# Counting the ranks of a router on VectorE instead of TensorE, in a one-core transformer block

## The chip, the cores and the metric

The kernel runs on one core of a Trainium2 chip. The metric is the device time of one execution in microseconds (us), lower is better. Five engines work side by side, each with its own in-order queue: TensorE (PE in the rows; PEld is its weight load), VectorE (DVE), ScalarE (ACT), GpSimd (POOL) and SyncE (SP, which here only starts transfers). They wait for one another through semaphores.

## What is computed

A transformer block on 8 batches of 512 tokens with 256 features: an adaptive layernorm, an attention block, a second layernorm, and a feed-forward part that ends in five steps of a spiking neuron. The attention has a light branch (windows of 64 tokens, all tokens) and a heavy branch (256 routed query tokens against 256 routed key tokens). What matters for the change is the routing: each token gets a score, and the 256 tokens with the largest scores are picked, in the order of their scores.

```
def route(rt, num):
    scores = jnp.einsum('bnd,d->bn', x, rt)
    idx = jnp.argsort(scores, axis=-1)
    ...
    sel_s, sel_i = (cs[:, -num:], idx[:, -num:])
    sel_s = sel_s + jax.lax.stop_gradient(1.0 - sel_s)
    return (sel_s, sel_i)
sq, iq = route(rt_q, NQ)
skv, ikv = route(rt_kv, NKV)
rq = jnp.take_along_axis(x, iq[:, :, None], 1)
rkv = jnp.take_along_axis(x, ikv[:, :, None], 1)
```

There are two routings for each batch (queries, r = 0, and keys, r = 1), 16 in all. The selected scores come out as 1, so only the token numbers count.

## The kernel before

The program is software-pipelined by hand. Its main part is a row of iterations, one for each batch: a "first" one, six equal ones ("loop", batches 1 to 6) and a "last" one, then a tail. An iteration has 24 slots, one for each pair of heads and block of queries (slots 0 to 15 light, 16 to 23 heavy; the last iteration has another order). In every slot each engine does its part of the attention, and then what tables put into that slot for other work:

- TensorE: the score products two slots ahead (`scores`), the units of the slot, the transposes of the probabilities (`turn`, L1243), and the products with the values of the slot before (`attend`).
- VectorE: `invert` (L1509), `minimum` (L1499 to L1503), `copy_out` (L1516), its share of the units, and then the row stages of the slot.
- ScalarE: a copy of the transposed probabilities, the exponentials, its share of the units, and the normalisation.
- GpSimd: gathers and scatters of rows by token number, reciprocal roots, and a few elementwise parts, at slots named in `POOL_SLOTS`.

`turn` of slot s waits for `copy_out` in slot s of VectorE, so the two engines can't drift apart by more than about a slot. A slot's end on TensorE comes either when its own products are through or when `copy_out` is.

The tables `FIRST_UNITS`, `SLOT_UNITS` and `LAST_UNITS` name the units of each slot. K, Q, V and NK, NQ, NV are projections of the light branch (6 products, L1059), HQ, HK, HV those of the heavy branch, FC and YA the two halves of the feed-forward part (L1059, L1190; FD is VectorE's part of it), LO and HO output projections (L1113, L1118), HT, ZT and Z3 transposes (L1091, L1123, L1128; Z3 turns the normalised rows of the feed-forward part), WF and WP preparations of weights. Units other than FD and YA share two PSUM banks, which alternate in the order of the table; a unit that is next for a bank waits until its last user is drained. `FIRST_ROWS`, `ROW_STAGES` and `LAST_ROWS` name VectorE's row stages: `stats1`, `center`, `modulate`, `add`, `stats3`, `norm3` and so on.

The routing for the next batch goes through these steps, each in a slot given by the tables: `router` (VectorE, four reductions to scores), SR (TensorE spreads the scores over all partitions, ScalarE copies them to `score_row`), `compare` (VectorE: for each of the four token tiles one row block of 0 and 1 of greater or equal, and a small one for ties, 11 instructions in two stages a and b), RK (TensorE sums these blocks over the partitions by 20 products with a column of ones, so the ranks land in PSUM), VectorE's part of RK (ranks to SBUF, then four instructions that mark, for each place of 256, which token holds it: `spots`), IX (TensorE: 16 products of `spots` with the token numbers, split in a low and a high part so that they are exact), VectorE's copy to `picks`, and then GpSimd's `pick`, which gathers the rows. The gathered rows are needed by HT at the start of the next iteration.

## Time and profile before

| | |
|---|---|
| median of 3 runs | 890.96 us (890.9 to 891.18) |
| the profiled execution: its own time | 887.45 us |
| the profiled execution: span from first to last instruction | 885.4 us |
| mean granted TensorE clock in it | 0.984 of full speed |

The profiled execution ran 3.5 us below the median of the timed runs, and its span is 2.05 us shorter than its own time; what lies outside the span belongs to the start and the end of the execution.

### The profile page before, as it was taken

Reading aid. Unit: us, or ns where it says so; the run is one execution under the profiler, and the core shown is the slowest. Engines: PE = TensorE matmul, PEld = TensorE weight load, DVE = VectorE, ACT = ScalarE, POOL = GpSimd, SP = SyncE. Lnnn points to the kernel's source line nnn. Section 1 sums busy time; section 2 is a strip of 40 time slices with the busy share of each in tenths; the row PEclk is TensorE's granted clock in tenths of the full one; section 3 lists DMA queues with packets and bytes.
Section 4 is the critical chain, followed back from the end, with each engine's and each line's share of the span. In section 5 each row is a group of like instructions: output and inputs, shape, how many; then the busy total and the mean of one; then the engine's idle time right before and its main releaser. Section 6 shows DMA issues by size and latency. Waiting matters only on the chain.

```text
span 885.4 us, 23955 instructions
## 1 busy us (share of the span) xinstructions
PE 820.1 (93%) x9170; PEld 622.8 (70%) x9170; DVE 586.1 (66%) x1740; ACT 612.7 (69%) x1738; POOL 206.5 (23%) x267
## 2 busy tenths in 40 slices
PE   4786889999999999999999999999999999999976
PEld 1464667678776777778776777677776777767766
DVE  6586763786568756786567756786567766453565
ACT  2355676788667886788667876787767886688633
POOL 3103021220241224120331224120222223200343
PEclk9798999999999999999999999999999999999998
DMA  9400030200022001310022000320022000210110
GB/s 317 148 31 26 4 100 13 91 26 2 26 75 82 25 14 39 102 54 2 26 67 91 25 14 25 97 67 8 21 71 91 25 14 25 61 49 1 37 31 24
DMA packets 32847, 45.35 MB, mean 51 GB/s; under 512 B 3304, under 2 KB 28144, under 8 KB 32512
## 3 DMA queue, kind: packets, MB, share of 16 engines
q1 hardware_dynamic: 29616, 37.53, 12.9%
q0 software_dynamic: 2304, 6.29, 2.3%
q8 instruction: 74, 1.21, 0.6%
q14 instruction: 37, 0.30, 0.1%
q10 hardware_dynamic: 816, 0.00, 0.0%
HBM read 32.52 MB, written 14.97 MB: 54 GB/s over the span
## 4 chain that ended last, share of the span: by engine, by line
PE 76%; DVE 6%; ACT 3%; issue 2%; POOL 1%; DVEq 0%; POOLq 0%; ACTq 0%
PE ps_unit L1059 30%; PE ps_y L1190 10%; PE ps_turned L1243 7%; PE ps_unit L1113 5%; PE ps_scores L1217 4%; PE ps_turned L1265 4%; PE ps_turned L1280 4%; PE ps_unit L1118 3%; PE ps_scores L1226 3%; DVE hn L1474 1%; PE ps_turned L1270 1%; DVE spikes L1491 1%; PE ps_unit L1123 1%; PE ps_unit L1152 1%; DVE loT L1516 1%
## 5 line engine op out<-in xcount | busy, mean ns | idle before, releaser
L990 ACT ACTIVATE probs<-ps_scores,row_min 128x192 f32<-128x192 f32 (+2 forms) x384 | 161.1, 425 | 101.5 <-DVE row_min L1499 54.0
L1000 ACT ACTIVATE probs<-probs,row_inv 128x192 f32<-128x192 f32 (+2 forms) x384 | 155.6, 456 | 0.4 <-DVE row_inv L1509 0.4
L1059 PE MATMUL ps_unit<-xT,wqkv 128*128 128x512 f32 x384 | 109.3, 422 | 2.7 <-POOL xT L798 1.7
L1499 DVE TENSOR_REDUCE row_min<-ps_scores 128x2 f32<-128x512 f32 (+1 forms) x128 | 78.6, 614 | 49.9 <-PE ps_scores L1226 24.3
L1243 PEld LDWEIGHTS ps_turned<-ident,probs 64*128 64x128 f32 x1280 | 56.0, 139 | 75.2 <-issue 65.6
L1190 PE MATMUL ps_y<-wprojT,hid_parts 128*128 128x256 f32 x768 | 104.2, 284 | 1.4 <-POOL hid_parts L563 0.9
L1190 PEld LDWEIGHTS ps_y<-wprojT,hid_parts 128*128 128x128 f32 x768 | 96.5, 188 | 10.0 <-issue 5.8
L1243 PE MATMUL ps_turned<-ident,probs 64*128 64x64 f32 x1280 | 81.5, 238 | 21.5 <-DVE loT L1516 19.1
L1059 PEld LDWEIGHTS ps_unit<-xT,wqkv 128*128 128x128 f32 x384 | 70.8, 194 | 29.5 <-issue 15.5
L1059 PE MATMUL ps_unit<-h_parts,wfcT 128*128 128x512 f32 x336 | 90.1, 403 | 0.1
L1008 ACT ACTIVATE probsT<-ps_turned 128x384 f32<-128x384 f32 x128 | 61.9, 484 | 21.9 <-PE ps_turned L1270 21.9
L990 ACT ACTIVATION_READ_ACCUMULATOR probs<-ps_scores,row_min 128x1 f32 x384 | 75.5, 197 | 0.0
L1217 PE MATMUL ps_scores<-kT,qT 64*64 64x192 f32 (+1 forms) x1024 | 71.3, 320 | 4.0 <-ACT probs L990 3.2
L1516 DVE TENSOR_REDUCE loT<-ps_turned 128x128 f32<-128x256 f32 x128 | 53.4, 417 | 27.1 <-ACT probsT L1008 19.6
L1059 PEld LDWEIGHTS ps_unit<-h_parts,wfcT 128*128 128x128 f32 x336 | 58.9, 188 | 13.9 <-issue 3.9
L1012 ACT ACTIVATE probsT<-ps_turned 128x512 f32<-128x512 f32 x64 | 37.9, 592 | 43.2 <-PE ps_turned L1280 42.3
L1113 PE MATMUL ps_unit<-wo_light,loT 128*128 128x256 f32 x256 | 62.0, 386 | 0.6 <-DVE loT L1516 0.6
L1265 PE MATMUL ps_turned<-probsT,v 64*64 64x128 f32 x1024 | 58.0, 297 | 0.3 <-DVE loT L1516 0.3
L798 POOL TENSOR_TENSOR xT<-full,xT 128x512 fp32r<-128x512 f32 x14 | 18.0, 1287 | 163.7 <-DVE xT L1429 163.7
L963 ACT ACTIVATE hid<-ps_unit 128x512 f32<-128x512 f32 (+1 forms) x72 | 39.7, 551 | 23.8 <-PE ps_unit L1059 22.5
L1113 PEld LDWEIGHTS ps_unit<-wo_light,loT 128*128 128x128 f32 x256 | 47.1, 189 | 11.7 <-issue 5.4
L1059 PE MATMUL ps_unit<-wqkv,xT 128*128 128x512 f32 x192 | 54.5, 420 | 0.1
(175 smaller groups left out, 1588.2 us busy)
## 6 DMA issues: line engine op xcount, KB each, us to landing
xa<-in_L_attn_x SPq DMA_DIRECT2D x8, 512.0 KB, 4.2
normed_rows<-hn SPq DMA_DIRECT2D x8, 512.0 KB, 3.0
lx<-in_L_attn_x SPq DMA_DIRECT2D x8, 512.0 KB, 3.9
out_x<-spikes SPq DMA_DIRECT2D x16, 256.0 KB, 2.2
hn<-routed_out SPq DMA_DIRECT2D x7, 512.0 KB, 4.1
routed_out<-zero_rows SPq DMA_DIRECT2D x14, 256.0 KB, 4.2
full<-mod_rows SPq DMA_DIRECT2D x7, 256.0 KB, 4.3
gate_a<-mod_rows SPq DMA_DIRECT2D x8, 128.0 KB
```

Of the source, the lines that this page charges most:

```text
L963: act.activation(hid_relu[:, i % 2, cols], ps[:, cols], ACT.Relu).then_inc(free, 1)
L990: ins = act.activation(probs[:, probs_buffer(n), probs_columns(s, part)], ps_scores[:, part, lo:hi], ACT.Exp, bias=row_min[:, n % 3, part: ...
L1000: ins = act.activation(rows, rows, ACT.Identity, scale=row_inv[:, n % 3, part:part + 1])
L1008: act.activation(probsT[:, 0:6 * W].rearrange("p (i c n) -> p c i n", i=3, c=2), ps_pT[:, :, 0:3 * W].rearrange("p c (i n) -> p c i n", i= ...
L1059: ins = pe.matmul(ps, w(wi, k, w_cols), a(ai, k, a_cols), start=(n == 0), stop=(n == 3 * KD - 1))
L1113: ins = pe.matmul(ps[:, 0:D], loT[:, p, i * P:(i + 1) * P], wo_light[:, p, :], start=(p == 0), stop=(p == PAIRS - 1))
L1190: ins = pe.matmul(ps_y[t // 2][:, (t % 2) * D:(t % 2 + 1) * D], hid_parts[hi][:, i % 2, t * P:(t + 1) * P], wprojT[wi][:, f, :], start=(f ...
L1217: ins = pe.matmul(ps_scores[c * W:(c + 1) * W, w, lo:hi], qT[heads[h], p % 2, query:query + W], kT[heads[h], p % 2, first_key + lo:first_k ...
L1243: ins = pe.transpose(ps_pT[:, c, i * W:(i + 1) * W], probs[rows, probs_buffer(n), run * P:(run + 1) * P], ident[rows, rows])
L1265: ins = pe.matmul(ps_oT[halves[h], g, :], v[halves[g], m, cols[h]], both, start=True, stop=m == (T - 1, 0)[g])
L1499: ins = dve.tensor_reduce(row_min[:, n % 3, :], ps_scores[:, :, lo:hi], AX.X, ALU.min)
L1516: dve.tensor_reduce(dst[:, p, m * P:(m + 1) * P], ps_oT.rearrange("p g n -> p n g"), AX.X, ALU.add).then_inc(oT_copied, 1)
```

## The change

The ranks no longer come from TensorE. Each of VectorE's 11 compare instructions of a routing also adds up what it writes along the row, and gives the sum to a column of the new tile `counts` (accumulator output). A new row stage `spots0` or `spots1` sums the three counts of each tile (one small reduction, `rank`), waits for it, and then makes `spots` as before; the table of places now runs downwards, since the sums along the row count the tokens above and not those below. The unit RK is gone from the tables, with its 20 products, its turn at a PSUM bank and VectorE's drain of it. IX takes the low and the high part of the token numbers as two columns of one product (8 products in place of 16), and VectorE adds the two columns when it makes `picks`.

All tables of units, of row stages and of GpSimd's slots are made anew, for every iteration. The blocks of 0 and 1 are still written, though only the sums are used. The diff, with the tables cut to the lines that matter below (a row of `0` and `1` behind a name is the routing or the tile; a name with a leading 0 belongs to batch 0):

```diff
@@ -56,29 +56,29 @@
 SLOT_UNITS = {
...
-    9: [("HQ", 0), ("Z3", 0), ("Z3", 1)],
-    10: [("HK", 0), ("FC", 0)],
...
-    13: [("FD", 2), ("HK", 1), ("FC", 3), ("RK", 0)],
...
+    9: [("Z3", 0), ("HK", 0), ("Z3", 1)],
+    10: [("FC", 0), ("HQ", 0)],
...
+    13: [("FD", 2), ("HK", 1), ("FC", 3)],
...
@@ -89,43 +89,42 @@
...
 ROW_STAGES = {
...
-    3: ["center_a"],
-    4: ["center_b"],
-    5: ["modulate"],
...
+    4: ["center_a"],
+    5: ["center_b", "modulate"],
...
-    14: ["norm2", "compare1a"],
...
+    13: ["norm2", "spots0"],
+    14: ["compare1a"],
...
@@ -135,56 +134,57 @@
 FIRST_UNITS = {
...
-    9: [("WF", 2), ("WF", 3), ("HT", 0), ("HT", 1)],
...
+    9: [("HT", 0), ("HT", 1)],
...
@@ -322,7 +322,6 @@
-        ones_bf = sb("ones_bf", [P, 2], BF16)
@@ -353,6 +352,7 @@
+        counts = sb("counts", [P, 2, T, 3])
@@ -477,6 +477,7 @@
+        ranked = sem("ranked")
@@ -707,7 +708,7 @@
-            pool.memset(ones_bf[:, :], 1.0).then_inc(consts_made, 1)
+            pool.memset(counts[:, :, :, :], 0.0).then_inc(consts_made, 1)
@@ -717,7 +718,7 @@
-            pool.iota(places[:, :], pattern=[[1, SEL]], base=0, channel_multiplier=0,
+            pool.iota(places[:, :], pattern=[[-1, SEL]], base=SEL - 1, channel_multiplier=0,
@@ -1151,14 +1152,6 @@
                     for t in range(T):
                         ins = pe.transpose(ps[:, t * P:(t + 1) * P], score[:, i, t:t + 1].to_broadcast([P, P]),
                                            ident[:, :])
-                elif kind == "RK":
-
-                    pe.wait_ge(compared, 2 * b + 3 + i)
-                    for t in range(T):
-                        for j in range(T):
-                            pe.matmul(ps[:, t:t + 1], greater[:, j, t * P:(t + 1) * P], ones_bf[:, 0:1],
-                                      start=(j == 0), stop=False)
-                        ins = pe.matmul(ps[:, t:t + 1], tie[:, t, :], ones_bf[:, 0:1], start=False, stop=True)
                 elif kind == "IX":
 
                     if b == -1 and i == 0:
@@ -1166,9 +1159,8 @@
                     pe.wait_ge(spotted, 2 * b + 3 + i)
                     for q in range(SEL // P):
                         for t in range(T):
-                            for j in range(2):
-                                ins = pe.matmul(ps[:, q:q + 1], spots[:, t, q * P:(q + 1) * P], tokens[:, j, t:t + 1],
-                                                start=(t == 0 and j == 0), stop=(t == T - 1 and j == 1))
+                            ins = pe.matmul(ps[:, 2 * q:2 * q + 2], spots[:, t, q * P:(q + 1) * P], tokens[:, :, t],
+                                            start=(t == 0), stop=(t == T - 1))
                 elif kind == "FC":
                     made = KD * (b - 1 + i // FT) if i % FT == 0 else None
                     f, cols = chunk_tokens(segment, i)
@@ -1410,16 +1402,32 @@
                     if r == 1:
                         wait_drained(dve, segment, n - 1, ("0IX" if n == 0 else "IX", 0))
                     dve.wait_ge(score_ready, 2 * n + r + 1)
+                    if n == 0 and r == 0:
+                        dve.wait_ge(consts_made, 6)
                 for j in tiles:
                     s = score[:, r, j:j + 1]
                     e = (j + 1) * P
-                    dve.tensor_scalar(greater[:, j, 0:e], score_row[:, 0:e], s, None, ALU.is_gt)
+                    dve.tensor_scalar(greater[:, j, 0:e], score_row[:, 0:e], s, None, ALU.is_gt, ALU.add,
+                                      accum_out=counts[:, r, j, 0:1])
                     if j < T - 1:
-                        dve.tensor_scalar(greater[:, j, e:N], score_row[:, e:N], s, None, ALU.is_ge)
+                        dve.tensor_scalar(greater[:, j, e:N], score_row[:, e:N], s, None, ALU.is_ge, ALU.add,
+                                          accum_out=counts[:, r, j, 1:2])
                     ins = dve.scalar_tensor_tensor(out=tie[:, j, :], in0=score_row[:, j * P:e], scalar=s,
-                                                   in1=later[:, :], op0=ALU.is_equal, op1=ALU.mult)
+                                                   in1=later[:, :], op0=ALU.is_equal, op1=ALU.mult,
+                                                   accum_out=counts[:, r, j, 2:3])
                 if tiles.stop == T:
                     ins.then_inc(compared, 1)
+
+            def spot(segment, n, r):
+
+                dve.wait_ge(compared, 2 * n + r + 1)
+                dve.tensor_reduce(rank[:, r, :], counts[:, r, :, :], AX.X, ALU.add).then_inc(ranked, 1)
+                if n == 0 and r == 0:
+                    dve.wait_ge(tokens_made, 3)
+                dve.wait_ge(ranked, 2 * n + r + 1)
+                for t in range(T):
+                    ins = dve.tensor_scalar(spots[:, t, :], places[:, :], rank[:, r, t:t + 1], None, ALU.is_equal)
+                ins.then_inc(spotted, 1)
 
             def high_part(segment, b, unit):
                 kind, i = unit
@@ -1538,15 +1546,6 @@
                             out=hT[1][:, i, k, :], in0=ps[:, k * SEL:(k + 1) * SEL], scalar=gamma_cols[:, 1, k:k + 1],
                             in1=hT[0][:, i, k, :].bitcast(F32), op0=ALU.mult, op1=ALU.subtract)
                     ins.then_inc(free, 1)
-                elif kind == "RK":
-                    ps, free = drain(segment, b, u)
-                    dve.tensor_scalar(rank[:, i, :], ps[:, 0:T], float(N - SEL), None, ALU.subtract).then_inc(free, 1)
-                    if early_one and i == 0:
-                        dve.wait_ge(tokens_made, 3)
-                    wait_drained(dve, segment, b, u)
-                    for t in range(T):
-                        ins = dve.tensor_scalar(spots[:, t, :], places[:, :], rank[:, i, t:t + 1], None, ALU.is_equal)
-                    ins.then_inc(spotted, 1)
                 elif kind == "IX":
                     ps, free = drain(segment, b, u)
                     n = b + 1
@@ -1554,7 +1553,9 @@
                         dve.wait_ge(picked[i], 32 * (n - 1))
                         if i == 0:
                             dve.wait_ge(ho_spread, 32 * (n - 1))
-                    dve.tensor_copy(picks[:, n % 2, i, :], ps[:, 0:SEL // P]).then_inc(free, 1)
+                    with nc.allow_low_precision(reason="sums of whole numbers under N into integers"):
+                        dve.tensor_reduce(picks[:, n % 2, i, :], ps[:, 0:2 * (SEL // P)].rearrange(
+                            "p (q j) -> p q j", j=2), AX.X, ALU.add).then_inc(free, 1)
                 elif kind in ("LO", "LX"):
                     ps, free = drain(segment, b, u)
                     n = light_batch(segment, b, u)
```

TensorE's program in the first of the six equal iterations, slot 13 (heavy key projection, one block of the feed-forward part, ranks, then `turn` and `attend`), before:

```order
L1059 MATMUL ps_unit<-hT,wkv_r 128x256 x12
L1059 MATMUL ps_unit<-h_parts,wfcT 128x512 x6
L1159 MATMUL ps_unit<-ones_bf,late 128x1 x4
L1161 MATMUL ps_unit<-ones_bf,late 128x1
L1159 MATMUL ps_unit<-ones_bf,late 128x1 x4
L1161 MATMUL ps_unit<-ones_bf,late 128x1
L1159 MATMUL ps_unit<-ones_bf,late 128x1 x4
L1161 MATMUL ps_unit<-ones_bf,late 128x1
L1159 MATMUL ps_unit<-ones_bf,late 128x1 x4
L1161 MATMUL ps_unit<-ones_bf,late 128x1
L1243 MATMUL ps_turned<-ident,probs 128x64 x6
```

and of the change:

```order
L1209 MATMUL ps_scores<-kT,qT 64x128 x2
L1060 MATMUL ps_unit<-hT,wkv_r 128x256 x12
L1060 MATMUL ps_unit<-h_parts,wfcT 128x512 x6
L1235 MATMUL ps_turned<-ident,probs 128x64 x6
L1257 MATMUL ps_turned<-probsT,v 64x128 x4
L1262 MATMUL ps_turned<-probsT,v 64x64 x2
```

The eight rows of ones_bf, 20 products, are gone; `turn` follows the feed-forward block directly.

VectorE's program in the same iteration from the end of slot 12 (the last two tiles of `compare`) into slot 13, before:

```order
L1416 TENSOR_SCALAR late<-late,score 128x512
L1419 SCALAR_TENSOR_TENSOR late<-late,score,later 128x128
L1509 RECIPROCAL row_inv<-row_sum 128x2
L1501 TENSOR_REDUCE row_min<-ps_scores 128x1
L1503 TENSOR_REDUCE row_min<-ps_scores 128x1
L1516 TENSOR_REDUCE loT<-ps_turned 128x128
L1576 TENSOR_TENSOR hid_parts<-hid,hid_parts 128x512
L1543 TENSOR_SCALAR rank<-ps_unit 128x4
L1548 TENSOR_SCALAR late<-places,rank 128x256 x4
```

and of the change:

```order
L1410 TENSOR_SCALAR late,counts<-late,score 128x512
L1415 SCALAR_TENSOR_TENSOR late,counts<-late,score,later 128x128
L1517 RECIPROCAL row_inv<-row_sum 128x2
L1509 TENSOR_REDUCE row_min<-ps_scores 128x1
L1511 TENSOR_REDUCE row_min<-ps_scores 128x1
L1524 TENSOR_REDUCE loT<-ps_turned 128x128
L1577 TENSOR_TENSOR hid_parts<-hid,hid_parts 128x512
L1393 TENSOR_SCALAR xa<-h,mv,rstd 128x256 x4
L1424 TENSOR_REDUCE rank<-counts 128x4
L1429 TENSOR_SCALAR late<-places,rank 128x256 x4
```

The compare instructions have `counts` as a second output, the rank comes from `counts` and not from PSUM, and the second layernorm of the row (L1393) has moved in ahead of it from slot 14.

VectorE's program in slots 4 and 5 of that iteration (`center_b` is the L1359 row of slot 4, `modulate` the L1371 row), before:

```order
L1509 RECIPROCAL row_inv<-row_sum 128x2
L1499 TENSOR_REDUCE row_min<-ps_scores 128x2
L1516 TENSOR_REDUCE loT<-ps_turned 128x128
L1565 TENSOR_TENSOR hid<-ps_unit,gate_a 128x256
L1359 SCALAR_TENSOR_TENSOR xa<-xa,mv,full 128x256 x2
L1509 RECIPROCAL row_inv<-row_sum 128x2
L1501 TENSOR_REDUCE row_min<-ps_scores 128x1
L1503 TENSOR_REDUCE row_min<-ps_scores 128x1
L1516 TENSOR_REDUCE loT<-ps_turned 128x128
L1371 SCALAR_TENSOR_TENSOR h<-xa,rstd,full 128x256 x4
```

and of the change:

```order
L1517 RECIPROCAL row_inv<-row_sum 128x2
L1507 TENSOR_REDUCE row_min<-ps_scores 128x2
L1524 TENSOR_REDUCE loT<-ps_turned 128x128
L1351 SCALAR_TENSOR_TENSOR xa<-xa,mv,full 128x256 x2
L1517 RECIPROCAL row_inv<-row_sum 128x2
L1509 TENSOR_REDUCE row_min<-ps_scores 128x1
L1511 TENSOR_REDUCE row_min<-ps_scores 128x1
L1524 TENSOR_REDUCE loT<-ps_turned 128x128
L1351 SCALAR_TENSOR_TENSOR xa<-xa,mv,full 128x256 x2
L1363 SCALAR_TENSOR_TENSOR h<-xa,rstd,full 128x256 x4
```

In slot 4 stood a drain of LO and the second half of `center`; now slot 4 holds the first half, and slot 5 the second half and `modulate` behind its three attention parts.

## Rows read from the trace of the kernel before

**Rows 1.** The page: busy time of TensorE, and its granted clock in 40 slices

```profile
PE 820.1 (93%) x9170; PEld 622.8 (70%) x9170; DVE 586.1 (66%) x1740; ACT 612.7 (69%) x1738; POOL 206.5 (23%) x267
...
PEclk9798999999999999999999999999999999999998
```

**Rows 2.** First, loop, last iteration: us, busy PE, PEld, DVE, ACT, POOL, clock, DMA

```profile
39.00:144.70 105.70, 87.21 (x1041) 63.53 (x1038) 70.82 (x233) 66.13 (x195) 19.10 (x25) 0.91 0.14 42
308.70:409.20 100.50, 98.47 (x1134) 75.55 (x1133) 69.64 (x212) 75.02 (x215) 24.57 (x30) 1.00 0.15 46
711.20:841.00 129.80, 126.95 (x1442) 97.78 (x1440) 69.99 (x183) 96.87 (x273) 24.55 (x24) 1.00 0.10 32
```

**Rows 3.** TensorE's waits in one loop iteration: total us, times, longest

```profile
PE ps_turned L1243 <- DVE loT L1516: 1.1, 2, 0.8
PE ps_unit L1128 <- ACT qT L898: 0.8, 1, 0.8
```

**Rows 4.** TensorE's waits in the first iteration, the two largest

```profile
PE ps_turned L1243 <- DVE loT L1516: 9.5, 8, 2.5
PE ps_unit L1091 <- DVE wfcT L1526: 3.4, 1, 3.4
```

**Rows 5.** Timeline of TensorE at a rank unit: start us, us, what

```profile
399.13 1.56 PE L1059 MATMUL ps_unit<-h_parts,wfcT 128*128 128x512 f32 x6
400.54 0.25 PE L1159 MATMUL ps_unit<-ones_bf,late 128*128 128x1 bf16 x4
...
401.03 0.16 PE L1161 MATMUL ps_unit<-ones_bf,late 128*128 128x1 bf16 x1
401.12 0.40 PE L1243 MATMUL ps_turned<-ident,probs 64*128 64x64 f32 x6
```

**Rows 6.** Timeline of TensorE at an index unit

```profile
330.18 0.55 PE L1170 MATMUL ps_unit<-tokens,late 128*128 128x1 bf16 x16
330.66 0.28 PE L1243 MATMUL ps_turned<-ident,probs 64*128 64x64 f32 x2
```

**Rows 7.** Timeline of VectorE in slots 12 and 13: compare, copy_out, rank

```profile
394.66 0.29 DVE L1416 TENSOR_SCALAR late<-late,score 128x128 bf16<-128x128 f32 x1
...
397.42 0.35 DVE L1419 SCALAR_TENSOR_TENSOR late<-late,score,later 128x128 bf16<-128x128 f32 x1
397.68 0.16 DVE L1509 RECIPROCAL row_inv<-row_sum 128x2 f32<-128x2 f32 x1
...
398.23 0.41 DVE L1516 TENSOR_REDUCE loT<-ps_turned 128x128 f32<-128x256 f32 x1
...
401.23 0.16 DVE L1543 TENSOR_SCALAR rank<-ps_unit 128x4 f32<-128x4 f32 x1 [1.98 <-PE ps_unit L1161]
```

**Rows 8.** Groups by line and shape: busy us, mean ns of one

```profile
L1416 DVE TENSOR_SCALAR late<-late,score 128x512 bf16<-128x512 f32 x16 | 7.7, 479 | 0.0
...
L1488 DVE TENSOR_SCALAR spikes<-ps_y 128x512 f32<-128x512 f32 x16 | 11.0, 685 | 2.1 <-PE ps_y L1190 2.1
...
L1419 DVE SCALAR_TENSOR_TENSOR late<-late,score,later 128x128 bf16<-128x128 f32 x64 | 22.1, 345 | 0.0
...
L990 ACT ACTIVATION_READ_ACCUMULATOR probs<-ps_scores,row_min 128x1 f32 x384 | 75.5, 197 | 0.0
```

**Rows 9.** Timeline of VectorE in the router: reductions with an accumulator read

```profile
387.99 0.42 DVE L1392 CUSTOM_DVE_ANT_0 routed<-h,router 128x256 bf16<-128x256 f32 x1
388.34 0.08 DVE L1392 DVE_READ_ACCUMULATOR2_ANT score<- 128x1 f32 x1
```

**Rows 10.** Timeline of VectorE in slots 3, 5 and 6 of a loop iteration

```profile
362.98 0.91 DVE L1359 SCALAR_TENSOR_TENSOR xa<-xa,mv,full 128x256 f32<-128x256 f32 x2
...
368.37 0.15 DVE L1509 RECIPROCAL row_inv<-row_sum 128x2 f32<-128x2 f32 x1
...
370.81 0.15 DVE L1509 RECIPROCAL row_inv<-row_sum 128x2 f32<-128x2 f32 x1
...
373.87 0.15 DVE L1509 RECIPROCAL row_inv<-row_sum 128x2 f32<-128x2 f32 x1
```

More of the change, by code:

```diff
@@ L137 @@
     19: ["y01", "y02"],
-    20: ["y03"],
-    21: ["y04", "y05", "y11"],
+    20: ["y03", "y04"],
+    21: ["y05", "y11"],
     22: ["y12", "y13"],
```

101 lines of the change are left out of this document (67 added, 34 removed), and 29 rows, old and new, of tables (LAST_UNITS, SLOT_UNITS).

## The prediction

> **What bounds the kernel now.** I read the page first, for who is busy: TensorE is, for 93% of the span, with VectorE at 66% and ScalarE at 69%, and its granted clock is near full except at the start and the end [rows 1]. A share over the whole span says little, so next come the stretches. In a loop iteration TensorE is busy 98.5 of 100.5 us at full clock, VectorE 69.6. The first iteration is another matter: 87.2 of 105.7 us, at a granted clock of 0.91, with VectorE at 70.8 [rows 2]. Last I read TensorE's own waits. In a loop iteration they come to about 2 us: 1.1 us in two waits for VectorE's `copy_out`, and 0.8 us at Z3 for a drain of its bank [rows 3]. In the first iteration it waits 9.5 us in eight pieces for `copy_out`, and 3.4 us at HT, behind the weight units in the same slot [rows 4]. So six of eight iterations go at TensorE's pace: what is taken from its queue is gained in full, and what VectorE is given costs nothing as long as `copy_out` stays early. In the first iteration VectorE's time counts as much as TensorE's.
>
> **What TensorE loses.** A rank unit starts at 400.54 and its last product at 401.03: 20 products in 0.49 us, 25 ns each; `turn` follows at 401.12 [rows 5]. I take 0.50 us for each of two units in an iteration. An index unit takes 0.48 us for 16 products [rows 6]; with half as many, and the end of the last one kept, it saves 0.2 us, twice. That a product with two columns takes as long as one with one is not shown by any row; the bounds are the same pace per product (0.2 us saved) and the same pace per column (nothing saved), and I take the first, since 25 ns for one column can't be the time of the column alone when 512 columns take some 0.23 us (six products, 1.41 us, rows 5). Together 2 x 0.50 + 2 x 0.2 = 1.4 us per batch. The Trainium skill (TensorE: Matmul & The Clock Gate, the section on 56 ns and not 53.3 ns) says that starts of matmuls never come closer than about 25 ns however few the columns; by it two columns are free, and the sum would be the same.
>
> **What VectorE is given.** A compare takes 394.66 to 397.68, 3.02 us for 11 instructions [rows 7]. Two things may lengthen it. First the pace: a TENSOR_SCALAR of 512 columns from SBUF takes 479 ns here, one from PSUM 685 ns [rows 8]. If the accumulator takes the faster pace away, 206 ns per 512 columns come on top, 0.8 us for the 2048 columns of a compare (seven instructions); the tie instructions already go at the slower pace, 345 ns for 128 columns. The bounds are 0 and 0.8, and I take 0.8. Second the reads of the accumulator, 11 of them. In the router a read is 0.08 us busy, but the next reduction starts at the same moment, so that it adds almost nothing [rows 9]; ScalarE's read is 197 ns [rows 8]. VectorE's own row is the nearer one: I take 0.02 us each, with 0 and 0.2 as bounds, 0.2 us for a compare. Sum: 1.0 us for a compare, bounds 0 and 3.0. The rank's reduction takes the place of the rank's drain (0.16 us, rows 7) and needs no product to be through.
>
> For the first of the two the Trainium skill (SBUF — State Buffer, Who interferes with whom) lists `tensor_scalar` among the operations that can use both ports, but "not the form that also writes out its accumulator". Here no row shows that form. By the rule the compare takes the slower pace, by the rows of before alone it could keep the faster one and cost 0.2 us; the total would then be 0 to 3 us lower, all of it in the first iteration.
>
> **What of it lies on the path.** In a loop iteration the long compare stands in slot 12. What waits for it is `copy_out` of slot 13, which ends at 398.64, while `turn` starts at 401.12 [rows 5, 7]: 2.48 us early, and 1.98 us when the rank unit ahead of `turn` is gone. 1.0 us is hidden there by the heavy projection and the feed-forward block. Without that cover it would cost 1.0 us an iteration. `norm2` moves to slot 13 and fills the 1.98 us in which VectorE waited for the ranks [rows 7], and takes itself out of slot 14, so the second routing's compare is not late either.
>
> The new tables give something back elsewhere. Slot 5 gets half of `center` on top of `modulate`: 0.83 us [rows 10] on 2.44 us (368.37 to 370.81), with 3.06 us of slot 6 behind it [rows 10], and all of that without idle time. TensorE's slots there hold one projection each. What is late next is `copy_out` of slots 6 and 7, and `turn` with it. The bounds are 0 (slot 4 loses as much and gives a lead) and 0.83; I take 0.35, which also stands for units that now follow one another less well. The wait at Z3 (0.8 us) goes, since HK now stands between the two Z3. But FC, which was behind HK, is now the first unit of slot 10, and needs both Z3 through ScalarE and VectorE (two steps each); I let it wait as long as was gained, so 0, with -0.8 as the other bound.
>
> Loop iteration: -1.4 + 0.35 = -1.05 us; six of them -6.3 us.
>
> First iteration: four rank and four index units, 2.8 us on TensorE, of which I count half (1.4), as VectorE ends many of its slots. Four compares at 1.0 us, of which I count 0.8, as they stand in such slots: +3.2. The weight units leave slot 9, so most of HT's 3.4 us goes: -2.5, with 0 as the bound if the transfer behind the gather is what comes last. Sum -0.7, between -6 and +5.
>
> Last iteration and tail have no routing; their tables move two neuron steps forward and LX back: -0.3, within 1.5 us either way.
>
> Total -6.3 - 0.7 - 0.3 = -7.3 us. The terms are from an execution of 887.45 us, whose like would come to 880.2; the median of the timed runs stands 3.5 us above it, and the same step from 890.96 us gives **883.7 us**. TensorE's granted clock stays as it is: full in the loop, broken by stretches at half in the first 90 us.
>
> **Rivals.** *The tables take waits out as well.* The Z3 wait goes for good (-0.8 x 6 = -4.8), and the first iteration, with weights moved out of the way, loses 4 us more of its 9.5 + 3.4 us of waits: about 875 us. For it: every table is new, and the 2 us of waits per iteration stand in two or three places only. Against: FC's inputs come through three engines.
>
> *VectorE takes it back.* Each accumulator read costs 0.08 us of VectorE's time, its busy time in rows 9, so a compare grows by 1.7 us. It is still under 1.98 in slot 13, but `norm2` and the rank behind it are then late for slot 14, and slots 5 to 8 lose their 0.83: -1.4 + 0.9 = -0.5 in the loop (-3.0), and 4 x 1.7 x 0.8 - 3.9 = +1.5, with new waits of about 1 us, in the first: 890.5 us. The Trainium skill (VectorE: DVE Perf Modes, Two Vector instructions with no wait between them) counts an operation with an accumulator output as two instructions, which speaks for a price of this kind.
>
> *The reads hold VectorE as long as ScalarE's are busy*, the slower side. With 0.2 us each a compare grows by 3.0 us. In slot 13 that is 1.0 us over the cover, and the loop gains -1.4 + 0.35 + 1.0 = 0; the first iteration gets 4 x 3.0 x 0.8 - 3.9 = +5.7: 896.4 us. It decides from about 0.15 us a read. Against it: VectorE's own reads of rows 9 add nothing between two starts.
>
> **How the numbers follow.** Forecast 62%, waits out as well 17%, VectorE takes it back 14%, reads like ScalarE's 7%. About 0.2%, 1.8 us, is what a measurement of this kernel can tell from no change. The forecast and the first rival are faster (79%), and a small part of the second (3%); most of the rest of the second lies within 0.2% (10%), and the third with the last of the second is slower (8%). The range leaves out the third rival and the ends of the other two: 875.5 to 890.
>
> **What would show it.** Right: a loop iteration of about 99.4 us, TensorE still busy for all but 2 us of it, no rows of one column, index units of 0.25 us; compare instructions of 512 columns at about 690 ns with reads that don't move the next start, and `copy_out` of slot 13 still about 1 us ahead of `turn`. Wrong: TensorE's waits for `copy_out` above 2 us per loop iteration, above all in slots 6 to 8 and 13 to 14 (VectorE is then the bound), or FC waiting in slot 10 for more than the Z3 gap had cost, or a first iteration longer than 106 us.

## The result, and the profile after

The changed kernel takes 888.06 us (median of 9 runs, 885.39 to 889.01), the kernel before on the same chip 890.51 us (9 runs): a ratio of 0.997, 95% interval 0.9958 to 0.9983. It is faster, by 2.5 us where 7.3 were forecast. Its profiled execution took 888.02 us with a span of 885.9 us. The one profiled before (887.45 us) stood 3.1 us under its own median, so the two traces differ by +0.5 us where the medians differ by -2.5. Another chip gave 0.9949 (0.9933 to 0.9964) for the same two kernels. What follows compares stretches of the traces.

The page, for the busy time of TensorE and its granted clock in 40 slices, to be held against [rows 1]:

```profile
PE 816.6 (92%) x8722; PEld 618.5 (70%) x8722; DVE 608.8 (69%) x1916; ACT 610.7 (69%) x1738; POOL 206.6 (23%) x267
...
PEclk9797889999999999999999999999999999999998
```

To set the eight iterations side by side I cut both traces at `turn` of slot 0; the last iteration ends at its own last `turn`. The windows of [rows 2] lie elsewhere: 711.2 to 841 holds 42 us of the sixth loop iteration, and 39 to 144.7 starts and ends too early, so before the change the first iteration is 108.1 us and not 105.7. Windows of the kernel before: first iteration, the third of the loop, the last (us, busy PE, PEld, DVE, ACT, POOL, granted clock, DMA share, GB/s):

```profile
41.88:149.98 108.10, 89.61 (x1083) 65.48 (x1082) 72.45 (x237) 68.01 (x201) 19.10 (x25) 0.93 0.12 36
351.04:451.55 100.51, 98.48 (x1133) 75.56 (x1133) 69.65 (x211) 75.03 (x215) 24.56 (x31) 1.00 0.15 46
753.46:842.52 89.06, 84.77 (x970) 65.07 (x970) 45.69 (x121) 67.42 (x192) 12.17 (x12) 1.00 0.12 38
```

The same of the changed kernel:

```profile
42.14:154.71 112.57, 91.22 (x970) 66.27 (x970) 76.87 (x281) 68.62 (x202) 18.76 (x25) 0.87 0.11 34
353.05:452.28 99.23, 97.43 (x1077) 74.47 (x1077) 72.84 (x233) 74.52 (x215) 24.67 (x31) 1.00 0.15 47
750.05:842.97 92.92, 84.60 (x971) 64.84 (x970) 45.26 (x121) 67.82 (x192) 12.19 (x12) 1.00 0.12 36
```

The six loop iterations take 8.1 us less (595.3 us for 603.5), the first takes 4.5 us more, the last 3.9 us more, start and tail 0.3 us more: +0.5 us. The loop gave more than forecast (6.3), the two ends took it back.

In the loop the steps of the prediction can be seen one by one. Timeline of TensorE, slot 13 and an index unit, the places of [rows 5, 6]:

```profile
400.29 1.54 PE L1060 MATMUL ps_unit<-h_parts,wfcT 128*128 128x512 f32 x6
401.76 0.40 PE L1235 MATMUL ps_turned<-ident,probs 64*128 64x64 f32 x6
...
406.38 0.35 PE L1162 MATMUL ps_unit<-tokens,late 128*128 128x2 bf16 x8
406.60 1.66 PE L1182 MATMUL ps_y<-wprojT,hid_parts 128*128 128x256 f32 x12
```

`turn` follows the feed-forward unit with nothing between, and an index unit lasts 0.22 us. Timeline of VectorE, the place of [rows 7]:

```profile
395.92 0.35 DVE L1410 TENSOR_SCALAR_CACHE_REDUCE late<-late,score 128x128 bf16<-128x128 f32 x1 [0.20 <-ACT late L946]
396.19 0.08 DVE L1410 DVE_READ_ACCUMULATOR late<-late,score 128x1 f32 x1
396.19 0.61 DVE L1413 TENSOR_SCALAR_CACHE_REDUCE late<-late,score 128x384 bf16<-128x384 f32 x1
...
400.09 0.16 DVE L1517 RECIPROCAL row_inv<-row_sum 128x2 f32<-128x2 f32 x1
...
400.62 0.41 DVE L1524 TENSOR_REDUCE loT<-ps_turned 128x128 f32<-128x256 f32 x1
...
401.55 0.73 DVE L1393 TENSOR_SCALAR xa<-h,mv,rstd 128x256 f32<-128x256 f32 x2
```

The operation behind the compare starts 4.17 us after its first one, where it was 3.02: 1.15 us more (the expectations below count to the end of the last read, 4.25 and 1.23). A read of the accumulator starts together with the instruction after it. `copy_out` ends at 401.03, 0.73 us ahead of `turn` at 401.76, and `norm2` stands right behind. The pace, groups by shape as in [rows 8]:

```profile
L1410 DVE TENSOR_SCALAR_CACHE_REDUCE late<-late,score 128x512 bf16<-128x512 f32 x16 | 11.8, 740 | 0.0
...
L1410 DVE TENSOR_SCALAR_CACHE_REDUCE late<-late,score 128x384 bf16<-128x384 f32 x16 | 9.7, 604 | 0.0
...
L1410 DVE DVE_READ_ACCUMULATOR late<-late,score 128x1 f32 x64 | 5.2, 82 | 0.0
```

740 ns for 512 columns, 479 before. TensorE's waits in this loop iteration [rows 3]:

```profile
PE ps_turned L1235 <- DVE late L1524: 0.9, 1, 0.9
PE ps_unit L1060 <- DVE hT L1545: 0.3, 1, 0.3
PE ps_unit L1129 <- ACT full L935: 0.2, 1, 0.2
PE ps_turned L1235 <- DVE loT L1524: 0.2, 1, 0.2
```

The two longest waits of before are gone, Z3's 0.8 us for `qT` and the 0.8 us for `copy_out` of slot 11; Z3 still waits 0.2 us, and 0.3 us (V 3 in slot 1) and 0.2 us (`copy_out` of slot 3) are new. So is one of 0.9 us in slot 20; more of it below.

In the first iteration the waits, as in [rows 4], have another shape:

```profile
PE ps_turned L1235 <- DVE loT L1524: 12.3, 9, 3.9
PE ps_unit L1162 <- DVE wprojT L1534: 2.3, 1, 2.3
PE ps_unit L1162 <- DVE late L1429: 1.8, 1, 1.8
```

HT's 3.4 us are gone, as forecast. But the wait for `copy_out` one slot later grew from 2.0 to 3.9 us: HT's drains and the eight reductions of the two `router` stages stand ahead of it on VectorE, and slot 10 has lost HK 0, whose 12 products (1.7 us) covered part of them. And 4.1 us stand at the two early index units. These wait for different things:

```profile
62.95 0.34 PE L1162 MATMUL ps_unit<-tokens,late 128*128 128x2 bf16 x8 [1.78 <-DVE late L1429]
...
79.44 0.37 PE L1162 MATMUL ps_unit<-tokens,late 128*128 128x2 bf16 x8 [2.31 <-DVE wprojT L1534]
```

The first waits for its spots. The second doesn't: its spots are ready at 76.6 us, and it starts when VectorE has drained a weight unit (79.4), whose PSUM bank it needs. Windows of that iteration around two of the stretches in which TensorE waited:

```profile
90.00:96.00 6.00, 1.51 (x18) 1.22 (x22) 4.93 (x24) 2.59 (x10) 0.96 (x3) 0.90 0.00 0
96.00:100.00 4.00, 3.94 (x58) 2.65 (x50) 2.37 (x7) 3.29 (x12) 0.00 (x0) 0.50 0.28 93
...
117.00:120.00 3.00, 1.45 (x32) 0.90 (x24) 3.00 (x13) 2.31 (x9) 0.00 (x0) 0.79 0.01 3
120.00:125.00 5.00, 5.00 (x44) 3.90 (x40) 3.13 (x13) 2.71 (x9) 0.00 (x0) 0.50 0.01 3
```

TensorE is busy 1.5 of 6 us, then its clock is at the lower level (0.50 granted, 1.2 GHz) while it has work nearly without a gap (3.94 of 4 us). In the first trace of before no such stretch lay behind 93 us. That is no mark of the change, though: the other trace of before (`before_again`, below) was at the lower level from 88 to 98 and from 122 to 129 us, and `after_again`, the changed kernel on that chip, at no time between 104 us and the tail.

In the last iteration TensorE is as busy as before (84.6 us) and waits more. Its timeline, the rows with a wait in slots 6 to 11:

```profile
773.19 0.40 PE L1235 MATMUL ps_turned<-ident,probs 64*128 64x64 f32 x6 [0.72 <-DVE loT L1524]
779.69 1.06 PE L1129 MATMUL ps_unit<-ident,hn 128*128 128x128 f32 x8 [0.91 <-DVE hn L1482]
783.26 2.00 PE L1060 MATMUL ps_unit<-h_parts,wfcT 128*128 128x512 f32 x6 [1.20 <-DVE h_parts L1440]
793.86 0.46 PE L1235 MATMUL ps_turned<-ident,probs 64*128 64x64 f32 x8 [1.02 <-DVE late L1524]
```

Before, the same slots held one wait of 0.35 us, so 3.5 of the 3.9 us stand here. Two of the four waits (2.1 us) lie on one chain: `norm3` (`hn`), Z3, the parts of FC's input (`h_parts`), FC. In both tables slot 9 holds nothing but FC 0; in the new one slot 8 too holds nothing but the two Z3, where HV 1 stood ahead of them. The other two (1.7 us) are waits for `copy_out` of slot 6 and of slot 11, which has lost its projection Q 2 to slot 10.

### The profile page after: what moved, and what is told of

The parts are those of the page before. It is cut to its first block, busy times and chain, and to the rows that moved or that the text cites. A ratio compares the mean times of both kernels' runs of the same rounds, so it can differ in the third digit from the quotient of the medians.

```text
span 885.9 us, 23218 instructions
## 1 busy us (share of the span) xinstructions
PE 816.6 (92%) x8722; PEld 618.5 (70%) x8722; DVE 608.8 (69%) x1916; ACT 610.7 (69%) x1738; POOL 206.6 (23%) x267
## 4 chain that ended last, share of the span: by engine, by line
PE 66%; DVE 11%; ACT 4%; issue 3%; another core or an unknown queue 1%; DMA 0%; POOL 0%; DVEq 0%; ACTq 0%; POOLq 0%; SPq 0%
PE ps_unit L1060 26%; PE ps_y L1182 10%; PE ps_turned L1235 6%; PE ps_unit L1114 5%; PE ps_turned L1257 4%; PE ps_scores L1209 3%; PE ps_unit L1119 3%; PE ps_scores L1218 3%; DVE spikes L1499 3%; PE ps_turned L1272 3%; ACT probs L991 2%; DVE row_min L1507 1%; PE ps_turned L1262 1%; DVE bn L1333 1%
## 5 line engine op out<-in xcount | busy, mean ns | idle before, releaser
L1060 PE MATMUL ps_unit<-xT,wqkv 128*128 128x512 f32 x384 | 106.5, 415 | 1.5 <-DVE xT L1440 1.0
L1182 PE MATMUL ps_y<-wprojT,hid_parts 128*128 128x256 f32 x768 | 106.4, 288 | 0.5 <-DVE hid_parts L1577 0.3
L1060 PE MATMUL ps_unit<-h_parts,wfcT 128*128 128x512 f32 x336 | 92.1, 405 | 1.9 <-DVE h_parts L1440 1.2
```

The lines of the kernel that those rows point to most:

```text
L1060: ins = pe.matmul(ps, w(wi, k, w_cols), a(ai, k, a_cols), start=(n == 0), stop=(n == 3 * KD - 1))
L1182: ins = pe.matmul(ps_y[t // 2][:, (t % 2) * D:(t % 2 + 1) * D], hid_parts[hi][:, i % 2, t * P:(t + 1) * P], wprojT[wi][:, f, :], start=(f ...
```

## The experiments

Sixteen runs stand in four groups, each on one chip with the kernel before beside it; some repeat a kernel on another chip. The ratios are of medians, the iterations' times (us) of one trace each, cut as above, with the third iteration for the loop. One trace says little about a first iteration: first_tables_before, counting_alone and loop_tables_new have the same one on the same chip, and took 118.1, 118.1 and 116.5 us; last_again and pick_earlier 110.9 and 109.9. What follows the last iteration takes 42.9 to 43.0 us in twelve of the traces of this document and 44.1 to 44.3 in the other six (loop_tables_new, counting_alone, spots_first, fillers_again, pick_earlier, pick_fillers). The edits are to the changed kernel unless said otherwise.

| run | chip | ratio to before, 95% | first | loop | last |
|---|---|---|---|---|---|
| last_tables_before | a | 0.9933 (0.992 to 0.9946) | 111.8 | 99.17 | 89.3 |
| first_tables_before | a | 1.0039 (1.0027 to 1.0052) | 118.1 | 99.2 | 92.5 |
| loop_tables_new | a | 0.9998 (0.9985 to 1.001) | 116.5 | 99.23 | 89.5 |
| counting_alone | a | 1.0023 (1.0012 to 1.0035) | 118.1 | 99.17 | 90.0 |
| outputs_added | b | 1.006 (1.0044 to 1.0076) | 110.5 | 100.7 | 89.3 |
| two_columns | b | 0.9989 (0.9977 to 1.0002) | 108.4 | 99.80 | 89.1 |
| spots_first | b | 0.9963 (0.9949 to 0.9977) | 114.2 | 98.33 | 89.3 |
| best_fillers | b | 0.9908 (0.9893 to 0.9923) | 109.4 | 98.3 | 89.3 |
| last_again | c | 0.9921 (0.99 to 0.9941) | 110.9 | 98.33 | 89.2 |
| fillers_again | c | 0.9901 (0.9882 to 0.9919) | 109.7 | 98.3 | 89.3 |
| pick_earlier | c | 0.9911 (0.9891 to 0.9931) | 109.9 | 98.25 | 89.3 |
| pick_fillers | c | 0.9905 (0.9885 to 0.9926) | 109.4 | 98.3 | 89.3 |
| before_again | d | 1.0006 (0.9992 to 1.0019) | 109.5 | 100.21 | 88.9 |
| after_again | d | 0.9949 (0.9933 to 0.9964) | 110.6 | 98.33 | 92.7 |
| outputs_again | d | 1.0074 (1.005 to 1.0097) | 110.5 | 100.67 | 89.3 |
| before_fillers | d | 0.9966 (0.9953 to 0.998) | 105.9 | 100.21 | 88.9 |

**Which tables.** Group a puts tables of before back.

```diff
-LAST_UNITS, LAST_ROWS, LAST_POOL_SLOTS of the change
+those of before                      # last_tables_before
-FIRST_UNITS, FIRST_ROWS, FIRST_POOL_SLOTS of the change
+those of before without RK, "0spots0" at the end of slot 3,
+"0spots1" first in slot 7, "spots0" in 13, "spots1" in 16
+                                     # first_tables_before; both: loop_tables_new
+SLOT_UNITS without RK, ROW_STAGES with "spots0" in 13 and
+"spots1" in 18, POOL_SLOTS of before # with both: counting_alone
```

> The changed kernel with the three tables of the last iteration (units, row stages, GpSimd's steps) as they were before the change. Theory A, the new tables of the last iteration themselves cost the 3.9 us by which it grew (93.0 us against 89.0, while TensorE is busy 84.7 us in both): the last iteration comes back to 89.0 to 89.3 us and the whole stands 6.3 us (ratio 0.993) below before. Theory B, the loop or the longer compares hand over late work to it: it stays at 92 us or more, ratio 0.997.

> The changed kernel with the tables of the first iteration as before, the rank units taken out and the stage that replaces them put right behind each compare's last half (slots 3, 7, 13 and 16). Theory A, the 4.5 us by which the first iteration grew come from its new tables, by idle stretches and the half clock behind them: it comes back to 108 us or 1 us less, and the whole stands 7 us below before (ratio 0.992). Theory B, they come from VectorE's compares, 4 x 1.23 us longer: it stays at 112 us or more, ratio 0.997, with any tables.

> Both of the above: the changed kernel with new tables in the six loop iterations alone. Theory A on both: about 11 us below before (ratio 0.987, 879.5 us). Theory B on both: ratio 0.997. The loop iterations stay at 99.2 us in either case.

> The new counting (accumulator outputs, no rank units, two-column index units) in the tables of before everywhere, the loop too: only the rank units are taken out, and the new stage stands in slots 13 and 18. Theory C, the loop's gain comes from TensorE's shorter queue and any order would give it: loop iteration 99.1 to 99.3 us. Theory D, the new order earns part of it (the Z3 wait of 0.8 us is gone, norm2 earlier): 99.8 to 100.1 us. With D a compare that is 1.2 us longer would show as copy_out waits in slots 13 to 15.

The last iteration is theory A: 89.3 us with its old tables, 93 with the new, and 3.7 thousandths of the ratio (0.9933 against 0.997, on two chips). The run puts all of its tables back at once, so which of the moves costs what is read from the waits alone. For the first iteration theory A falls: with the old tables it is not shorter but 6.3 us longer (118.1 for the 111.8 of last_tables_before, on the same chip). Theory B gave no such number either (ratio 0.997; it was 1.0039). The new tables earn time there; the new counting in the old order costs 7 to 10 us (116.5 and 118.1 against 109.5 and 108.1 in the two traces of before). counting_alone is theory C on this chip, 99.17 us a loop iteration whichever tables, and yet slower than before as a whole, by its first iteration. So on chip a the loop's gain came from the counting: TensorE is busy 97.16 us an iteration in the old order and 97.44 in the new, for 98.5 before. And there the change without new tables is no gain: 1.0023 with the counting alone. Whether the new order earns something in the loop where slot 20 has no wait was not run.

**The counting's parts.** In group b, outputs_added and two_columns are edits to the kernel before.

```diff
# outputs_added (and on the greater-or-equal and the tie instruction likewise)
-dve.tensor_scalar(greater[:, j, 0:e], score_row[:, 0:e], s, None, ALU.is_gt)
+dve.tensor_scalar(greater[:, j, 0:e], score_row[:, 0:e], s, None, ALU.is_gt, ALU.add,
+                  accum_out=counts[:, r, j, 0:1])
# two_columns: the index unit and its drain as in the change, nothing else
# spots_first: loop_tables_new, and in the first iteration
-3: ["low1", "center_a", "0spots0"]
+3: ["0spots0", "low1", "center_a"]
```

> The kernel before with the accumulator outputs added to its compares and nothing else: the counts are written and nobody reads them, TensorE counts as before. VectorE's 4.25 us compares without the shorter queue. The prediction's step, the longer compare is hidden in the loop and 0.8 of it shows in the first iteration: loop 100.5 us as before, first iteration 108.1 + 4 x 1.23 x 0.8 = 112.0 us, whole +3.9 us (ratio 1.004). Rival, the delay also brings longer stretches of TensorE at half clock: first iteration 114 us or more, ratio 1.006 or more. Second rival, the loss in the first iteration is not the compares' but the new stage's place: first iteration under 110 us.

> The kernel before with the two-column index units alone (8 products for 16, and a reduction for the copy of their result). The prediction's step, a product of two columns takes as long as one of one: an index unit takes 0.22 us for 0.42, loop iteration 100.1 us for 100.5, whole 2.5 to 3 us less (ratio 0.997). Rival, the pace goes by columns: 100.5 us, ratio 1.0.

> Like loop_tables_new, but in slot 3 of the first iteration the stage that makes the spots stands ahead of low1 and center_a, where the rank's drain of before stood. Theory E, of the 8.4 us that the first iteration lost with the tables of before, 2.2 us are TensorE waiting for these spots in slot 4: the first iteration comes back from 116.5 to 114 us or less, the whole to ratio 0.997. Theory F, the compares' length alone makes it late: 116 us and ratio 1.0 as before this move.

two_columns: an index unit costs 0.20 us less, 0.40 an iteration (99.80 against 100.21 of before_again, another chip with the same behaviour). The ratio missed its 0.997: it shows 1.1 us less, with 2.0 less and 0.2 more as the ends, where six iterations make 2.4. The median holds the first iteration too, which varies by as much. outputs_added: the first iteration takes 1.0 to 2.4 us more (against 109.5 and 108.1, the two traces of before), less than the 3.9 of the prediction's rule and less than the rival's 6. But the ratio went the rival's way, since the loop lost too. spots_first: the first iteration came back by 2.3 us (114.2 from 116.5), as theory E said, though these are single traces on two chips. Firmer is the wait itself: the index units wait 1.3 us for their spots in place of 2.8. The ratio of 0.9963 owes most to the loop, 98.3 us on this chip for 99.2. spots_first stays 3.7 us above outputs_added, and the clock doesn't explain it as a whole, since both have 0.89 granted on average. It moves time within the iteration. Timeline of spots_first, two projections behind a wait of 1.7 us:

```profile
128.81 2.90 PE L1060 MATMUL ps_unit<-xT,wqkv 128*128 128x512 f32 x6 [1.72 <-POOL xT L799]
131.51 1.05 PE L1060 MATMUL ps_unit<-wqkv,xT 128*128 128x512 f32 x2
```

and the same two of outputs_added, whose clock was up:

```profile
127.03 1.63 PE L1060 MATMUL ps_unit<-xT,wqkv 128*128 128x512 f32 x6 [1.70 <-POOL xT L799]
128.50 1.56 PE L1060 MATMUL ps_unit<-wqkv,xT 128*128 128x512 f32 x6
```

From the first projection to the second 2.70 us against 1.47, so 1.2 us here. What the other 2.5 us are was not measured.

**The clock.** Filling products go ahead of `turn`, into a bank that nobody reads in the first iteration:

```diff
+if first:
+    for _ in range(FILLERS.get(s, 0)):
+        pe.transpose(ps_y[0][:, 0:P], ident[:, :], ident[:, :])
 turn(n, slot_at(s, last))
# best_fillers, fillers_again: last_tables_before with
# FILLERS = {3: 12, 4: 4, 6: 20, 10: 32, 14: 8, 15: 10, 16: 14, 19: 8}
# before_fillers: before with {3: 12, 5: 10, 6: 20, 8: 6, 10: 18, 14: 7}
```

> Like last_tables_before (the fastest so far, 883.1 us), with 108 products of 128 columns added to TensorE's queue in the first iteration, in the slots where it waited longest for copy_out (3, 4, 6, 10, 14, 15, 16 and 19), written to a bank that nobody reads then. Theory G, the half clock of the first iteration (0.87 granted on average, some 29 us at half) follows TensorE's idle stretches and costs time: with the idle filled the clock stays up behind 95 and behind 119 us, the first iteration loses 3 us or more, ratio 0.990 or less. Theory H, the half clock does not depend on it, or what runs under it is bound by VectorE: ratio 0.993 as without fillers, or above it where a filler makes turn late.

best_fillers came 2.5 thousandths under last_tables_before, but on a chip where the loop iteration takes 98.3 us and not 99.2. The two kernels together on one chip:

> The same kernel as last_tables_before, once more, to stand on one chip with the next three. There the loop iterations took 99.2 us with a 0.8 us wait of TensorE for copy_out of slot 20, behind a row minimum that VectorE starts 1.4 us after GpSimd's second gather instruction; in spots_first, with the same loop tables on another chip, 98.3 us without it, the minimum starting 0.01 us ahead of that instruction. Theory I, which of the two comes first is settled by some 10 ns and differs between chips: either value, the same one in all iterations. Whole: ratio 0.993 with the wait, 0.987 without it if the kernel before is not touched by it.

> The same kernel as best_fillers, beside last_again on one chip. Theory G, the half clock behind idle stretches costs the first iteration time: 2 to 5 us less than last_again, first iteration 109.4 us against 111.8. Theory H, the lead of best_fillers was the loop's alone (98.3 us for 99.2): equal to last_again within 0.2%.

> The kernel before with 73 filling products of 128 columns in front of turn in slots 3, 5, 6, 8, 10 and 14 of its first iteration. If the half clock costs time before the change too: 1 to 3 us less (ratio 0.998 or less). If only the longer waits of the changed kernel bring a half clock that matters: ratio 1.0 within 0.002.

The result lies between the two theories: fillers_again has 876.2 us against 877.96 (both at 6 runs, 874.98 to 877.11 and 875.62 to 878.54), first iteration 109.7 against 110.9, granted clock 0.95 against 0.88. The second pair on this chip, pick_fillers against pick_earlier below, has 876.68 against 877.02 us, first iteration 109.4 against 109.9. The four together make it 1.3 us (medians of 12 runs each). Behind 85 us and up to the tail the clock stayed at the upper level in all three traces with these fillers, so the remedy did what it should to the clock, and time hardly followed. (last_again missed its 0.987 with 0.9921, though its loop had 98.3 us: the kernel before took 884.2 us on this chip, for 889.0 on chip a.) Before the change the same remedy brings more: ratio 0.9966, some 3 us, first iteration 105.9 against 109.5 us, clock 0.97 against 0.87. So the half clock is a cost of the first iteration before the change, and its length goes with it: 105.9 us at 0.97 granted, 108.1 at 0.93, 109.5 at 0.87. By this the clock isn't what the change lost there. With fillers in both (not in the same slots, and on two chips) 109.7 stands against 105.9 us, nearly as far apart as without them on the first chip, and on chip d the two kernels had nearly the same clock (0.87 and 0.88) and 1.1 us between them. What is left goes with VectorE's longer work (76.9 us busy for 72.5) and the waits shown above; a share for each was not measured in the new tables.

**The wait of slot 20.** The same loop tables gave 99.2 us on chip a and 98.3 on b. pick_earlier moves one of GpSimd's two gathers out of slot 20:

```diff
# pick_earlier: last_again with
-"norm_rows": 15, "pick0": 20, "pick1": 20}
+"norm_rows": 15, "pick0": 18, "pick1": 20}   # pick_fillers: with the fillers
```

> Like last_again, but GpSimd's first gather of routed rows (pick0) stands in slot 18 of the loop iterations, as before the change, and no longer in slot 20 beside pick1. Theory I, the wait of slot 20 is the meeting of this gather with VectorE's row minimum: it is gone, loop iteration 98.3 us, 5 us less than last_again where that one has the wait, nothing where it hasn't. Rival, the minimum waits for something else in slot 20: loop iteration as in last_again, 99.2 us.

> Both, pick0 in slot 18 and the 108 filling products in the first iteration: the sum of the two effects, 98.3 us a loop iteration and 109.4 us the first, ratio 0.989 or less on any chip.

> The kernel before, unchanged, profiled on the chip of the next three. Loop iteration 100.5 us as in its first profile, or 99.7 us where a wait of 0.8 us is missing on this chip; ratio 1.0 by definition.

> The changed kernel, unchanged, on the same chip. If the loop's gain is TensorE's shorter queue alone (1.4 us) its iteration is 1.3 to 1.4 us under before_again's. If the wait of slot 20 is there (99.2 us) and before_again has 99.7 us, the gain is 0.5 us; if it is absent in both, 98.3 against 99.7 or 100.5 us. Whole: ratio 0.997, last iteration 92.9 and first 112.5 us whatever the chip.

> The kernel of outputs_added (accumulator outputs that nobody reads, added to the kernel before). The prediction's step: nothing is lost in the loop, its iteration is before_again's to 0.1 us. Rival: the longer compares cost the loop something too, 0.5 us or more an iteration (its profile showed 100.7 us on a chip where two_columns took 99.8).

Chip c had no such wait, so pick_earlier could show nothing there (877.02 against 877.96 us), and whether it helps on the other kind is not settled; pick_fillers is no better than fillers_again and missed its 0.989. But chip d shows both kernels side by side. Windows of before_again:

```profile
42.09:151.59 109.50, 93.97 (x1081) 68.92 (x1080) 72.33 (x237) 68.01 (x201) 20.01 (x25) 0.87 0.12 35
352.02:452.23 100.21, 98.46 (x1135) 75.57 (x1134) 69.89 (x211) 74.92 (x215) 24.60 (x31) 1.00 0.15 47
```

and of after_again:

```profile
42.56:153.19 110.63, 89.80 (x970) 65.33 (x970) 76.94 (x281) 68.06 (x202) 19.07 (x25) 0.88 0.11 35
349.53:447.86 98.33, 97.43 (x1079) 74.49 (x1078) 72.88 (x233) 74.71 (x215) 24.76 (x31) 1.00 0.15 47
```

Loop 1.9 us less an iteration (-12.0 in all six), first +1.1, last +3.8: the spans differ by 6.6 us, the medians by 4.7 us, and the ratio is 0.9949 where the first chip had 0.997. outputs_again has 0.46 us more in a loop iteration than before_again, with no faster queue to pay for it: with the rank unit kept the compare is not hidden, and the rival's size is nearly met. Timeline of outputs_again in slot 13:

```profile
402.19 1.56 PE L1060 MATMUL ps_unit<-h_parts,wfcT 128*128 128x512 f32 x6
...
403.23 0.60 ACT L911 ACTIVATE kT<-ps_unit 128x512 f32<-128x512 f32 x1
...
403.88 0.25 PE L1160 MATMUL ps_unit<-ones_bf,late 128*128 128x1 bf16 x4
```

The rank unit starts 1.69 us after the feed-forward unit, where it was 1.41 [rows 5]. It doesn't wait for the compare, which was through at 401.9, but for its PSUM bank: ScalarE copies that bank's last product (`kT`, from HK) until 403.83, and the rank unit starts at 403.88. In before_again this copy was done 0.6 us ahead of the rank unit. So the longer compare comes to TensorE by way of VectorE's row minima, which stand behind it, and of ScalarE's exponentials, which wait for them and stand ahead of the copy. That is 0.3 of the 0.46 us; the change has no rank unit and no such wait in slot 13.

The fastest kernel of all, fillers_again (the change, the last iteration's tables of before, and the fillers), is at 0.9901 of before.

## Why the prediction was wrong, step by step

**TensorE's loss was right.** The rank units are gone, an index unit is down by 0.20 us, as forecast, and two_columns confirms it by itself. In the old order TensorE is busy 1.3 us less an iteration (counting_alone, 97.16 for 98.46), near the 1.4 forecast. The products of an index unit start 25 ns apart behind the first two (40 ns), with two columns as with one. The Trainium skill (TensorE: Matmul & The Clock Gate, Wait — 56ns, not 53.3ns?) states 25 ns as the least distance of two starts, and these traces agree.

**VectorE's price was right in kind, a little small.** The pace: the seven instructions gain 261, 192, 194, 128, 128, 63 and 47 ns, each the difference of its group's mean in the two traces (740 - 479 for 512 columns), 1.01 us for a compare, where I had 0.8 from PSUM's 685 ns. The 11 reads add the rest of the 1.15, about 0.01 us each. The Trainium skill (SBUF — State Buffer, Who interferes with whom) sets the form that writes out its accumulator apart from plain `tensor_scalar`, and the measured pace agrees. Its other rule (VectorE: DVE Perf Modes, Two Vector instructions with no wait between them), two instructions for one, is what the rows list, but the second costs next to nothing here. The rivals on costly reads fall with that.

**The cover in slot 13 held.** 0.73 us are left of it. With the rank unit kept the compare costs the loop 0.46 us, mostly by the bank that this unit waits for; the prediction had looked at `copy_out` alone.

**The loop's tables: the forecast was too careful.** The 0.35 us to be lost came, but not where it was put: slots 5 to 8 wait for nothing, slot 3 waits 0.2 us for `copy_out`, and TensorE is busy 0.3 us more than in counting_alone, as its units follow one another less well. FC's wait, set equal to what Z3 gained, isn't there: Z3, V 3 and slot 3 wait 0.7 us together where Z3 and slot 11 waited 1.5. With this the loop gains 1.9 us an iteration on chips without the wait of slot 20, near the rival *the tables take waits out as well*, and 1.3 with it, against 1.05 forecast.

**The first step that failed: in the first iteration "Sum -0.7" was +4.5 us, +1.1 on chip d.** The sum counted TensorE's and VectorE's shares and one wait. HT's wait went, as said, but what stood behind it was not free: the wait for `copy_out` of slot 10, which lost HK 0, grew by 1.9 us, one early index unit waits 1.8 us for its spots, which are now a stage behind the compare, and the other 2.3 us for a weight unit's bank. The four compares themselves were not under-priced: alone they cost 1.0 to 2.4 us here (outputs_added), for +3.2 in the sum. The clock was no part of the sum; it makes the two differences differ, since the first trace of before had 0.93 granted and the other 0.87. The bounds (-6 to +5) held it. The sign "a first iteration longer than 106 us" could tell nothing, as the kernel before has 108.1 us from `turn` to `turn`.

**The step that failed on both chips is "Last iteration and tail have no routing; their tables move two neuron steps forward and LX back: -0.3, within 1.5 us either way".** It was +3.9 us and +3.8, outside its own bounds, and by last_tables_before it is this iteration's tables alone. I had looked at the neuron steps and LX, and not at what stands between `norm3`, Z3 and FC (2.1 us of waits), nor at a projection moved out of a slot that VectorE ends. With that term at zero the change stands at 0.9933 and 0.9921 of before, 6 to 7 us faster: nearly what was forecast. On the first chip the rest is the loop's surplus of 1.8 us against the first iteration's 5.2; and 3.1 us are no step at all: the profiled execution of before stood that far under its median, so the forecast for the trace (-7.3 us) meets +0.5 and that for the median meets -2.5.

## What to carry to other kernels

When tables of order are made anew, read every table for its chains of dependent steps (here norm, transpose, parts, product) and ask which unit fills the time between two of them; a part of the program that loses nothing by the new operation can still lose most by its new order. An accumulator output was paid for here in the pace of its own instruction, not in the read. Whether a longer instruction is hidden is to be asked of every engine behind it in the chain, down to the PSUM bank that one of them frees. At a start where TensorE waits, its clock can cost time as well, and products that nobody reads are a cheap trial: 3 us here before the change, some 1 us after it.

## What the runs showed of the hardware

On some chips an engine that waits while GpSimd's gathers run starts late. Timeline of the changed kernel in slot 20 on the first chip, where ScalarE and VectorE both waited for products of TensorE (for VectorE the scores from 433.38 on):

```profile
432.64 1.12 POOL L776 DMA_INDIRECT routed<-normed_rows,picks  x1 [0.17 <-issue]
...
433.38 0.61 PE L1218 MATMUL ps_scores<-kT,qT 64*64 64x256 f32 x8
...
434.06 0.95 POOL L776 DMA_INDIRECT routed<-normed_rows,picks  x1 [0.30 <-issue]
...
434.79 0.60 ACT L1013 ACTIVATE probsT<-ps_turned 128x512 f32<-128x512 f32 x1 [3.89 <-PE ps_turned L1272]
435.52 0.69 DVE L1507 TENSOR_REDUCE row_min<-ps_scores 128x2 f32<-128x512 f32 x1 [3.85 <-PE ps_scores L1218]
```

The same place of after_again:

```profile
429.19 1.12 POOL L776 DMA_INDIRECT routed<-normed_rows,picks  x1 [0.17 <-issue]
...
429.93 0.61 PE L1218 MATMUL ps_scores<-kT,qT 64*64 64x256 f32 x8
430.23 0.60 ACT L1013 ACTIVATE probsT<-ps_turned 128x512 f32<-128x512 f32 x1 [2.79 <-PE ps_turned L1272]
430.61 0.69 DVE L1507 TENSOR_REDUCE row_min<-ps_scores 128x2 f32<-128x512 f32 x1 [2.40 <-PE ps_scores L1218]
```

VectorE starts 2.14 us after the start of the scores there and 0.68 us here, ScalarE 1.1 us later too, while TensorE itself runs on. In slot 20 of the loop VectorE started 1.35 to 1.48 us behind the second gather's start in every iteration on the first chip and on chip a, and -0.01 to 0.01 us on chips b, c and d, with the same tables. At the scatter of slot 3 before the change it was 1.43 to 1.48 us in the first trace and 0.42 to 0.45 us on chip d. Before the change a delay of this kind, at the scatter of slot 3, took 0.3 us an iteration (100.51 against 100.21 us), with the new tables 0.9 us in slot 20. So some 3.6 us of the loop's gain depend on the chip, and whoever compares two traces should see that they come from one chip. What is held up, the signal or the start, and whether GpSimd is the cause or only stands beside it, these traces don't tell; that `pick0` in slot 18 avoids it was not shown.
